# A decoder chain on one core: second cross attention with row maxima sent unit by unit, and a mixture of experts whose token table comes from one-hot products

## The reference, cut to what matters

```python
def _L1_xattn_ref(qkv, y):            # qkv: x as (16*16 heads, 8 channels, 512); y: the context, the same shape
    scale = 1.0 / math.sqrt(math.sqrt(ch))
    weight = jnp.einsum('bct,bcs->bts', q * scale, k * scale)      # 512 x 512 for each of 256 heads
    weight = jax.nn.softmax(weight, axis=-1)
    a = jnp.einsum('bts,bcs->bct', weight, v)                      # v = k = y

def _moe_forward(x, ...):             # 2048 tokens, 64 experts of width 128, top 4, capacity 64
    logits = flat @ router_w.T
    scores = softmax(logits); _, topk_idx = top_k(logits + router_bias, 4)
    topk_w = taken from scores, divided by their sum
    # pairs (token, expert) sorted by expert; the first 64 of each expert get a slot
    tok_table[e, slot] = token; w_table[e, slot] = weight
    xg = flat[tok_table]                                           # 64 experts x 64 rows
    y = (silu(xg @ gate_w.T) * (xg @ up_w.T)) @ down_w.T
    out = zeros.at[tok_table].add(y * w_table)
    # two shared experts of width 512 on all tokens (the dense part)
    out = out + sum over s of (silu(flat @ sh_gate) * (flat @ sh_up)) @ sh_down
```

## Time and profile before

| what | us |
|---|---|
| median of 3 runs | 3713.44 (3706.49 to 3716.21) |
| profiled execution | 3739.18, its span 3737.4, mean granted TensorE clock 0.906 |
| second cross attention, its maxima and body | 2388 to 3110 of the span |
| mixture, its first transpose | 3141.96 |
| first dense step of the mixture | from 3179.26 |
| experts | from 3362.36 |
| second dense half | from about 3558 |

### The profile page before, as it was taken

The page is one execution under the profiler, slowest core; times in us unless marked ns, Lnnn a source line. Parts: engine busy times, 40 slices in busy tenths (PEclk is TensorE's granted clock), DMA queues, the critical chain, the costliest instruction groups (busy, mean ns, idle before and its releaser), DMA issues. The chain is left out here.

```text
span 3737.4 us, 61006 instructions
## 1 busy us (share of the span) xinstructions
PE 3141.4 (84%) x21884; PEld 1811.7 (48%) x21884; DVE 2119.8 (57%) x2654; ACT 1529.9 (41%) x2642; POOL 810.0 (22%) x897
## 2 busy tenths in 40 slices
PE   7888674999949986999996999588888895979986
PEld 4343231333316654888885676122222223757765
DVE  3545444898823554344444344799999961731167
ACT  2221121577743322333331333078888894311121
POOL 3221053022210000110210245201111111151153
PEclk9999886699978997999998999689999997987998
DMA  2000166355431003453543132323333323358975
GB/s 81 27 30 24 38 196 179 88 153 141 126 111 47 29 3 107 127 157 121 153 149 98 51 92 77 92 75 96 100 99 100 97 89 99 112 131 282 388 215 154
DMA packets 383458, 423.79 MB, mean 113 GB/s; under 512 B 69105, under 2 KB 254961, under 8 KB 381954
## 3 DMA queue, kind: packets, MB, share of 16 engines
q1 hardware_dynamic: 221136, 258.92, 22.4%
q10 hardware_dynamic: 140546, 109.08, 9.7%
q0 software_dynamic: 21504, 51.98, 4.6%
HBM read 305.29 MB, written 113.99 MB: 112 GB/s over the span
## 5 line engine op out<-in xcount | busy, mean ns | idle before, releaser
L380 ACT ACTIVATE c_probs<-c_st 128x512 f32<-128x512 f32 x1536 | 834.3, 598 | 308.4 <-PE c_st L308 274.7
L421 DVE TENSOR_REDUCE c_maxes<-c_s 128x2 f32<-128x1024 f32 x768 | 905.2, 1217 | 82.4 <-PE c_s L289 78.1
L325 PE MATMUL c_o<-c_probs,c_v_aug 128*32 128x256 f32 x6144 | 509.2, 404 | 70.1 <-ACT c_o_raw L387 56.6
L289 PE MATMUL c_s<-c_k_st,c_q_st 48*128 48x512 bf16 (+1 forms) x1536 | 359.7, 465 | 116.7 <-DVE c_maxes L421 41.2
L308 PE MATMUL c_st<-c_q_st,c_k_st 51*128 51x512 bf16 (+1 forms) x1536 | 328.8, 404 | 5.2 <-DVE c_y L464 5.1
L289 PEld LDWEIGHTS c_s<-c_k_st,c_q_st 48*128 48x128 bf16 (+1 forms) x1536 | 103.5, 131 | 462.5 <-issue 222.2
L325 PEld LDWEIGHTS c_o<-c_probs,c_v_aug 128*32 128x32 f32 x6144 | 124.0, 109 | 335.6 <-issue 170.2
L308 PEld LDWEIGHTS c_st<-c_q_st,c_k_st 51*128 51x128 bf16 (+1 forms) x1536 | 156.0, 130 | 69.0 <-issue 27.6
L1869 ACT ACTIVATE a_probs<-a_sc 128x512 f32<-128x512 f32 x128 | 66.1, 603 | 281.6 <-PE a_sc L1747 281.6
L3011 DVE TENSOR_TENSOR f_w_lo<-f_w_raw,f_w_hi 128x1536 fp32r<-128x1536 f32 x64 | 117.2, 1831 | 105.0 <-ACT f_w_hi L2932 104.9
L2932 ACT ACTIVATE f_w_hi<-f_w_raw 128x1536 fp32r<-128x1536 f32 x64 | 95.2, 1488 | 89.7 <-PE f_out_ps L2883 62.0
(11 more groups left out here) (405 smaller groups left out, 5920.2 us busy)
## 6 DMA issues: line engine op xcount, KB each, us to landing
c_o_dram<-c_o_raw SPq DMA_DIRECT2D x96, 256.0 KB, 2.3
f_w_raw<-in_f_win ACTq DMA_DIRECT2D x96, 256.0 KB, 3.1
f_w_raw<-in_f_wup ACTq DMA_DIRECT2D x96, 256.0 KB, 3.3
f_w_raw<-in_f_wdown ACTq DMA_DIRECT2D x96, 256.0 KB, 3.5
f_x<-x_dram SPq DMA_DIRECT2D x48, 256.0 KB, 3.9
c_k_dram<-f_parts ACTq DMA_DIRECT2D x96, 128.0 KB, 2.5
c_q_dram<-a_parts SPq DMA_DIRECT2D x96, 128.0 KB, 2.4
c_q_st<-c_q_dram SPq DMA_DIRECT2D x128, 96.0 KB, 2.3
```

Of the source, the lines that this page charges most:

```text
L289: mm = nc.tensor.matmul(s1_ps[:, i, half, :], q_st[r:r + ROWS, s, i, tt * P:(tt + 1) * P], k_st[r:r + ROWS, s, i, :], start=True, stop=True)
L325: mm = nc.tensor.matmul(o_ps[32 * h:32 * h + 32, queries], v_aug[:, (j // NG) % NBS, st, (j % NG) * G + h, :], probs[:, (st * 4 + i * 2 + ...
L380: nc.scalar.activation(probs[:, e % 8, :], st_ps[:, st_bank(j, e), :], ACT.Exp).then_inc(exp_done, 1)
L421: nc.vector.tensor_reduce(maxes[:, jb % 2, :].rearrange("p (h r) -> p h r", h=2)[:, :, c], s1_ps[:, i, :, :], AX.X, ALU.max).then_inc(max_ ...
```

## The change

The first cross attention keeps the old function. The second goes to a copy, `cross_attention_by_unit`, with these differences:

```diff
-    AHEAD = NG + 2
+    AHEAD = 3
-    LAG = 2 if PROJ else 1
+    LAG = 2
-    RW = NG * 2 * KT
+    RW = 2 * KT
-    m_dram = nc.dram_tensor(f"{tag}_m_dram", (B, P, MP, 64), plain).ap()
+    m_dram = nc.dram_tensor(f"{tag}_m_dram", (UNITS, P, MP, 64), plain).ap()
-        m_t = sb(f"{tag}_m_t", [P, 64])
+        m_t = sb(f"{tag}_m_t", [P, 2, 64])
+                def send_max(it, j):                                  # SP, once a unit
+                    u = it * RING + j
+                    sp.wait_ge(m_stored[j % 2], 16 * (it * (RING // 2) + j // 2 + 1))
+                    if begun(u - 1):
+                        sp.wait_ge(st_full, (u - 2) * EXPS + 1)
+                    for half in range(2):
+                        for m in range(MP):
...
+                            sp.dma_start(dst, src[0:RW, :, :]).then_inc(m_ld[j % 2], 16)
+                def turn_max(it, j):                                  # VectorE, once a unit
+                    dve.wait_ge(max_done, 2 * KT * (u + 1))
+                    if begun(u - 1):
+                        dve.wait_ge(m_step, (u - 1) * STEPS)
+                    nc.vector.transpose(m_t[:, j % 2, :], maxes[:, j % 2, :]).then_inc(m_turned, 1)
+                def split_max(it, j):                                 # GpSimd, once a unit
+                    pool.wait_ge(m_turned, u + 1)
+                    if begun(u - 1):
+                        pool.wait_ge(m_ld[j % 2], 32 * MP * (it * (RING // 2) + j // 2))
+                    nc.gpsimd.tensor_copy(out[:, 0, :], whole).then_inc(m_step, 1)
+                    nc.gpsimd.tensor_tensor(rest, whole, out[:, 0, :], ALU.subtract).then_inc(m_step, 1)
+                    nc.gpsimd.tensor_copy(out[:, 1, :], rest).then_inc(m_step, 1)
+                    nc.gpsimd.tensor_tensor(out[:, 2, :], rest, out[:, 1, :], ALU.subtract).then_inc(m_step, 1)
+                    pool.dma_start(m_dram[bass.ds(u, 1), :, :, :].rearrange("o p m c -> p (o m) c"),
+                                   out.bitcast(plain)).then_inc(m_stored[j % 2], 16)
```

In the mixture:

```diff
-                for b in range(B):
-                    product(b)
-                    if b + 2 < B:
-                        transpose(b + 2)
-                gate_up(0)
+                product(0)
+                transpose(2)
+                product(1)
+                transpose(3)
+                product(2)
+                product(3)
+                gate_up(0)
+                transpose(4)
+                transpose(5)
+                tiles_from(4, 9)
+                gate_up(1)
+                tiles_from(9, B)
+                down(0)
-                    if n == 5:
+                    if n == 8:
                         pe.wait_ge(count_taken, 2)
+                    if n == 15:
+                        pe.wait_ge(table_odd, 1)
                     gate_up(n)
-                    if n == 4:
+                    if n == 7:
                         count(n)
+                    if n == 14:
+                        tokens_of_slots(n)
                     down(n - 1)
+                pe.wait_ge(silu_done, FIRST)
+                e_transpose(0)
                 down(FIRST - 1)
-                pe.wait_ge(silu_done, FIRST)
-                pe.wait_ge(hidden_done, FIRST)
-                pe.wait_ge(y_done, EARLY)
-                e_transpose(0)
+                def tokens_of_slots(n):                               # TensorE
+                    pe.wait_ge(spots_ready, 1)
+                    pe.wait_ge(silu_done, n)
+                    for k in range(TOPK):
+                        for b in range(B):
+                            mm = nc.tensor.matmul(gate_ps[0:CAP, (n + 1) % 2, 0:2 * E].rearrange("p (s e) -> p s e", s=2),
+                                                  spot[:, k, b, :], by_token[k][:, :, b, :],
+                                                  start=(k == 0 and b == 0), stop=(k == TOPK - 1 and b == B - 1))
-                for n in range(NSEL):
-                    nc.gpsimd.indirect_dma_start(
-                        table, bass.IndirectOffsetOnAxis(ap=slot_i[:, n:n + 1], axis=0),
-                        token[:, n // TOPK:n // TOPK + 1], None).then_inc(scattered, 16)
-                pool.wait_ge(table_ld, 16)
+                pool.wait_ge(table_even, 1)
+                pool.wait_ge(odd_placed, 16)
```

In the second dense half `add_rows` of a tile comes one step later (`j = n - FIRST - 1`), and the layer norm is in two parts:

```diff
-                def normalize(n, a):
+                def statistics(n, a):                                 # VectorE
                     nc.vector.bn_stats(stats[:, :], a).then_inc(ln_step, 1)
...
+                    nc.vector.tensor_scalar(mean_neg[:, i:i + 1], mv[:, i, 0:1], -1.0, None, ALU.mult).then_inc(ln_step, 1)
-                    dve.wait_ge(rstd_done, n + 1)
-                    nc.vector.tensor_scalar(x_new[:, n % 2, :], a, mv[:, 0:1], rstd[:, 0:1],
-                                            ALU.subtract, ALU.mult).then_inc(x_done, 1)
+                    nc.gpsimd.tensor_tensor(shift[:, i:i + 1], mean_neg[:, i:i + 1], rstd[:, i:i + 1], ALU.mult
+                                            ).then_inc(shift_done, 1)    # GpSimd, behind the power
+                def finish(n, a):                                     # ScalarE, a step later
+                    act.wait_ge(shift_done, n + 1)
+                    nc.scalar.activation(x_new[:, n % 2, :], a, ACT.Identity, bias=shift[:, n % 2:n % 2 + 1],
+                                         scale=rstd[:, n % 2:n % 2 + 1]).then_inc(x_done, 1)
```

More of the change, by code:

```diff
@@ L17 @@
 TWO_ONES = 1.0 + 2.0 ** -9 - 2.0 ** -16
+TWO_MINUS_ONES = -(1.0 + 0xBF80 / 2 ** 23)
 class Phase:
@@ L3437, in _, with tiles_from @@
                 pe.wait_ge(const_ld, CONSTS)
-                for b in range(B):
-                    product(b)
-                    if b + 2 < B:
-                        transpose(b + 2)
+                def tiles_from(first, last):
+                    for b in range(first, last):
+                        product(b)
+                        if b + 2 < B:
+                            transpose(b + 2)
+                product(0)
[4 more added lines that the diff above has]
+                product(3)
+                pe.wait_ge(h_hi_done, TOK)
+                pe.wait_ge(h_lo_done, TOK)
+                pe.wait_ge(logit_done, TOK)
+                gate_up(0)
[4 more added lines that the diff above has]
+                tiles_from(9, B)
                 pe.wait_ge(h_hi_done, B)
@@ L3562, in _ @@
                         load_weights(n + 4)
+                    j = n - FIRST - 2
+                    if 0 <= j < EARLY:
+                        finish(j, base[j % SLOT])
+                    elif EARLY <= j < EARLY + TOK:
+                        finish(j, y[:, j % TOK, :])
+                for n in range(B - TOK, B):
+                    finish(n, y[:, n % TOK, :])
             @block.vector
```

716 lines of the change are left out of this document (628 added, 88 removed).

## The result

The kernel after takes 3656.52 us (median of 4, 3644.06 to 3690.23), the one before 3709.97 on the same chips. The ratio is 0.9878 with a 95% interval of 0.9841 to 0.9914, which is 45 us less (32 to 59). The forecast was 3655. Stage by stage it was less good: of its five terms two came out, two were wrong, and the one for the experts was five times too small.

What follows compares the result with a forecast made beforehand. No engine bounds all stages: VectorE and ScalarE pace c1, TensorE leads the first dense half, DMA the experts, VectorE's chain the second half. -22 - 13 - 5 - 5 - 18 = -63 from median 3713.44, +5: 3655 us, range 3630 to 3680.

Steps and rivals of the forecast that it cites:

- first rival: Mixture's first half: VectorE bounds it, nothing gained before the experts and 5 lost behind them; 3675 us, chance 0.17.
- the second: Experts: they stay at full clock, 18 more of 26 us come back; 3637 us, chance 0.13.
- c1, -22: Second cross attention: 24 us less from running three units ahead instead of six, 2.4 more for per-unit work.
- -13 up to the last gate/up: Mixture, first product to last gate/up: scatter and idle stretch go, new products and waits come; 198.1 to 185.4 us.
- sum of 185.4: Mixture, first product to last gate/up: predicted length in us from tiles, dense steps, token products and waits.
- 1.5 for a colder clock: Mixture, tiles 4 to 15 between dense products: 1.5 us allowed for slower TensorE work.
- what is queued behind the waiting instruction: Second cross attention: check of work behind new SP and GpSimd waits; it claimed slack or spare buffers, no added time.
- -5 into the experts: Last gate/up to experts: first transpose ahead of the last down product overlaps its copy; 14 us becomes 9.
- -5 in the experts: Experts: fewer pairs at half clock after a shorter idle lead-in; 5 us less, between 0 and 26.
- -18 in the second half: Second dense half: steps fall from 9.87 to 8.80 us, first step by 9.7; 18 us less.
- end term of +1.4: Second dense half's end: 1.4 us added, beside a late row sum of 3.11 and norms overlapping by 1.
- the 5 us set aside for the hole: Mixture: 5 us added to the forecast because the 40 us low-TensorE stretch may partly belong to the profiled execution alone.

Runs made afterwards that it cites:

- no scatter: Kernel before, with 63 of the 64 scattered DMAs of the token table left out: ratio 0.9939, 23 us less.
- early transpose: Kernel before, with only the first transpose of expert rows moved ahead of the last down product: ratio 0.9988, 4 us less.
- later rows alone: Kernel before, second dense half's row sums one step later, layer norm left on VectorE: ratio 0.9969; that half took 167.6 us.

## Why the prediction was right, and where not

The total was right, and in part by luck. The sum had -13 - 5 - 5 = -23 us from the mixture's first product to the end of the experts, and the traces have 3.3 - 1.6 - 27.1 = -25, but by another way: nothing gained ahead of the experts, as in the first rival, though for other reasons, and all of it at the experts, as in the second.

- **c1, -22**: right (-23.3 in the trace, pace unchanged). The trip was mis-sized: 13.7 us on average and up to 19.5, instead of 10.5 to 12, because SP's issues took 5.2 us instead of 3.88 and other work stands ahead of them in its order. The prediction followed what is queued behind SP's new wait, and not the older wait ahead of it.
- **-13 up to the last gate/up**: wrong, +3.3 against the profiled run. Against its own sum of 185.4 the stretch took 201.4, 16 more, and the sum itself counts one down product of 2.8 too many (15 whole steps, where 14 down products stand ahead of the last gate/up). Up to the fourth step 6.4 more, 9 without that slip: the waits of the interleaved tiles came as charged (8.3 forecast, 8.1 idle), but the term "1.5 for a colder clock" was some 11. From there to step 14 2.8. At the token table 6.9: I had priced the products and their first wait, and missed that the token copies stand on VectorE behind a weight split which needs the down product behind the products. That is the step "what is queued behind the waiting instruction", not followed a second time. (The products themselves have 128 columns and not the 64 of the sum; 5.54 us against 5 is luck.)
- **-5 into the experts**: wrong, -1.6. The transpose waits 4.88 us for its gather, which GpSimd issues only when the last gate/up is done, since the rows land in the early tokens' memory. I had looked at the table and not at this second condition.
- **-5 in the experts**: mis-sized, -27 in this pair of traces; over all traces 167.5 to 180.4 with the one order against 178.7 to 196.0 with the other. I had tied the cold start to the hole; no scatter, with no hole, starts as cold, with pairs of 9.8 and 9.4 us. It was the order of the last three pieces of work. The 27 belong to the profiled execution, though: early transpose gives 4 us in the times, so for the average execution -5 may be near.
- **-18 in the second half**: right, -20.1, and by its terms: the first step fell by 9.7 us (9.7 forecast), the others from 9.87 to 8.7 (8.80). Its end term of +1.4 has no source in the sum, and neither has the part of the 9.7 over the two waits it names (4.41 and 3.3). The later rows alone gave 3.4, since without the norm's move the second step and the end give the first step's gain back.
- **Not in the sum**: 3.7 us less between c1's last copy and the mixture's first product, in all 9 traces with the new c1 (36.8 to 37.5 against 39.9 to 40.9 in the 5 with the old). Its cause was not tried.

The 63 us of the sum stand against 45 (32 to 59), so the sum itself was too large; the 5 us set aside for the hole went in the right direction, and so did taking the 63 off the median and not off the profiled run.

## What to carry to other kernels

A hole in a trace shows where a cost is paid in that execution, not what it is: take its suspected cause away, and also take away what it seems to hold up, before pricing it. Ask first whether the profiled execution is a usual one: here its time and its mean clock both said that it was not. When work is put between steps of a pipeline, follow each engine's order twice: the instruction that waits, then what stands behind it whose result is the next one's wait, and also what stands ahead of it. Price a new wait of TensorE with the clock behind it: here 6.7 us idle came with 11 us of slower matmuls. And look at what runs right ahead of a stage: it set the clock the experts started with.

## What the runs showed of the hardware

Beside GpSimd's products from SBUF, VectorE's operations from SBUF took longer (1.76 to 3.29 us, 1.67 to 4.96); VectorE's reductions from PSUM beside small GpSimd operations did not (1216 ns both ways). One unit's maxima took 15.6 us through DRAM and two queues, nearly four times its two landings, and most of the rest was SP's queue. Behind 6.04 us without work TensorE's next products took 1.97 us instead of 1.00, and behind 35.16 us idle a down product began at 0.63 us a matmul and ended at 0.39. Dense TensorE work beside 64 scattered DMAs ran at full speed in one trace, and in three it nearly stopped for some 30 us or more.
